# Expert rows stored in the tokens' order: plain loads instead of gathers, and shared experts in chunks of 256

## The reference

```
layer 1: h = norm(h + moe)   8 experts, top 2:  sum over e of gate[t,e] * (gelu(LN(x) w1[e] + b1[e]) w2[e] + b2[e])
layer 2: h = norm(h + moe)  16 experts, top 2:  sum over e of gate[t,e] * ((silu(x wg[e]) * (x wu[e])) wd[e])
                            + mean over s = 0, 1 of (silu(x shared_wg[s]) * (x shared_wu[s])) shared_wd[s]
layer 3: h = norm(h + moe)   8 experts, top 1:  p[t] * (relu(x wi[e]) wo[e])
```

## Time and profile before

| | |
|---|---|
| runs before | 2610.99, 2610.76, 2607.44 us, median 2610.76 |
| profiled execution | 2604.46 us, span on the core 2602.6 us, mean granted clock 0.884 |
| busy over the span | PE 2198.8 us (84%), DVE 1468.0 (56%), ACT 872.4 (34%), POOL 909.1 (35%) |
| bytes | HBM read 162.67 MB, written 63.28 MB |

### The profile page before, as it was taken

The page is one execution under the profiler, slowest core; times in us unless marked ns, Lnnn a source line. Parts: engine busy times, 40 slices in busy tenths (PEclk is TensorE's granted clock), DMA queues, the critical chain, the costliest instruction groups (busy, mean ns, idle before and its releaser), DMA issues. The chain is left out here.

```text
span 2602.6 us, 47198 instructions
## 1 busy us (share of the span) xinstructions
PE 2198.8 (84%) x17833; PEld 1944.9 (75%) x17833; DVE 1468.0 (56%) x3567; ACT 872.4 (34%) x1886; POOL 909.1 (35%) x828
## 2 busy tenths in 40 slices
PE   8999995689789858996998979998999995663598
PEld 7888884477678747994676769998999995552487
DVE  2676776746667764324999853332443226777424
ACT  0333435622244413333654431111111112576211
POOL 0333234700011062326777521310111116563546
PEclk9988996789999958998999989999999998755599
DMA  9500000070090055551000023001566651000354
GB/s 271 184 1 1 1 1 20 1 221 2 9 215 2 12 174 166 181 171 31 14 11 11 1 82 141 30 15 61 194 213 212 213 192 50 11 1 1 111 171 124
DMA packets 134490, 229.02 MB, mean 88 GB/s; under 512 B 15402, under 2 KB 105902, under 8 KB 127482
## 3 DMA queue, kind: packets, MB, share of 16 engines
q1 hardware_dynamic: 123642, 207.35, 25.1%
q0 software_dynamic: 10624, 18.66, 2.4%
HBM read 162.67 MB, written 63.28 MB: 87 GB/s over the span
## 5 line engine op out<-in xcount | busy, mean ns | idle before, releaser
L2623 POOL COPY bl_swiglu_w<-ahead_w2swiglu_w 128x1152 f32 x51 | 58.4, 1147 | 359.8 <-PE psum L2684 264.6
L2726 ACT ACTIVATE bl_swiglu_sg<-psum 128x384 f32<-128x384 f32 x102 | 50.0, 490 | 300.6 <-PE psum L2673 300.6
L2662 PE MATMUL psum<-bl_swiglu_xt,bl_swiglu_w 128*128 128x128 f32 x1224 | 147.3, 278 | 1.7 <-DVE bl_swiglu_hid L2763 1.1
L2662 PEld LDWEIGHTS psum<-bl_swiglu_xt,bl_swiglu_w 128*128 128x128 f32 x1224 | 145.5, 195 | 2.3 <-issue 2.3
L2753 DVE COPY bl_swiglu_xt<-psum 128x256 f32<-128x256 f32 x51 | 21.6, 424 | 198.4 <-PE psum L2643 198.4
L2623 POOL COPY bl_gelu_w<-ahead_w2gelu_w 128x1350 f32 x43 | 57.8, 1365 | 144.1 <-DVE bl_gelu_y L2785 131.0
L2738 ACT ACTIVATE bl_gelu_hid<-psum,bl_gelu_w 128x128 f32<-128x128 f32 x258 | 70.9, 377 | 110.4 <-POOL bl_gelu_w L2623 107.4
L2684 PE MATMUL psum<-bl_swiglu_w,bl_swiglu_hid 128*128 128x192 f32 x612 | 107.9, 327 | 0.0
L2988 ACT ACTIVATE shared_sg<-psum 128x432 f32<-128x432 f32 x66 | 35.0, 530 | 206.5 <-PE psum L2925 206.5
L2918 PE MATMUL psum<-tower_xT,shared_w 128*128 128x216 f32 x528 | 100.2, 347 | 0.6 <-ACT tower_xT L2982 0.6
L2684 PEld LDWEIGHTS psum<-bl_swiglu_w,bl_swiglu_hid 128*128 128x128 f32 x612 | 98.3, 191 | 0.1
(11 more groups left out here) (679 smaller groups left out, 6081.9 us busy)
## 6 DMA issues: line engine op xcount, KB each, us to landing
bl_swiglu_w<-in_swiglu_w SPq DMA_DIRECT2D x51, 1152.0 KB, 5.3
rows_in<-tower_fill SPq DMA_DIRECT2D x2, 13824.0 KB, 45.6
bl_gelu_w<-in_gelu_w SPq DMA_DIRECT2D x43, 576.0 KB, 4.1
bl_relu_w<-in_relu_w SPq DMA_DIRECT2D x25, 576.0 KB, 4.0
rows_last<-tower_fill SPq DMA_DIRECT2D x1, 14065.0 KB, 62.6
ahead_w2swiglu_w<-in_swiglu_w SPq DMA_DIRECT2D x1, 9216.0 KB
tok_x<-in_x SPq DMA_DIRECT2D x11, 648.0 KB, 12.5
ahead_w2gelu_w<-in_gelu_w SPq DMA_DIRECT2D x1, 5400.0 KB
```

What stands on the lines that cost most here:

```text
L2623: pool.tensor_copy(w2[:, n % DEEP], w2all[:, e, :].rearrange("p e n -> p (e n)")).then_inc(s_w2, 1)
L2662: pe.matmul(up_tile(n, j, i, side), w[:, o:o + 128], xt[:, n % 2, side, :], start=(i == 0), stop=False, skip_group_check=True)
L2726: act.activation(sg[:, j], bank_pair(n, j)[:, 0, 0:3 * BLOCK].rearrange("p (i n) -> p i n", i=3), ACT.Silu).then_inc(s_silu, 1)
```

## The change

- **One row format.** The DRAM array `rows_in` is 194 wide for all three layers and has one shelf more; `rows_last` and its clearing go. `h` gets a row pitch of 194 values. Column `NAME` of each row carries the token's number plus an epoch that differs by layer (`first_name`), `MORE` the first pick (relu: the factor).
- **Scatter in the blocks.** Gelu and SwiGLU lose SP's `store`. DVE computes for each of the 128 rows of a block where its result belongs (`addressed`): token number, plus 2304 if the row's expert is not the token's first pick; a row that holds no token of this layer goes to a spare row. POOL scatters `y` of block n - 4 behind its copy of block n. `y` has 4 buffers instead of 2. SP's next load of rows waits for the address step instead of the turn.
- **Plain loads in the combine.** `fetch` moves from POOL to SP: one transfer for a tile brings both results of its 108 tokens, two for the last tile. The first four stand ahead of all else in SP's stream of the stage. `slots`, `find_slots` and the slot arithmetic of the routes go; the block plan (`lay_blocks`) now runs on 128 partitions and also writes `mine`, the expert of each block on every partition.
- **Shared experts in chunks of 256.** 9 chunks for each expert, 18 iterations. Their sums are laid out by 128 rows, not by 108, so SP stores them to a DRAM array `rows_shared` and the SwiGLU stage loads them back in tiles of 108, behind the first three blocks' loads; `h` += `side` moves from block n to block n + 4. `GATES` moves from `NP + 6` to `NP + 5`.

The core of the diff:

```diff
@@ blocks, SP
                         if n >= XR:
-                            sp.wait_ge(c_y if last else p_T, n - XR + 1)
+                            sp.wait_ge(c_y if last else c_to, n - XR + 1)
...
                     S.arrived(sp, s_all)
+                    if glu:
+                        side, both = cst["side"], cst["both"]
+                        sp.wait_ge(cst["kept"], 16 * (TOK // (2 * BLOCK)))
+                        sp.dma_start(side[:, 0:NT - 1], both[0:(NT - 1) * T].rearrange("(t p) n -> p t n", p=T)).then_inc(cst["level"], 16)
...
                     for n in range(NB):
                         if n + DEEP < NB:
                             fetch_rows(n + DEEP)
                             fetch_weights(n + DEEP)
-                        if glu:
-                            store(n)
-                        elif n >= 3 and not last:
-                            store(n - 3)
@@ blocks, POOL
                     def scatter(n):
-                        x = n % KEPT
-                        pool.wait_ge(c_z, n + 1)
-                        pool.indirect_dma_start(out=cst["out"], out_offset=bass.IndirectOffsetOnAxis(ap=to[:, x:x + 1], axis=0),
+                        x, k = n % KY, n % KT
+                        pool.wait_ge(c_z if last else c_y, n + 1)
+                        pool.indirect_dma_start(out=out, out_offset=bass.IndirectOffsetOnAxis(ap=to[:, k:k + 1], axis=0),
                                                 in_=y[:, x, :], in_offset=None).then_inc(s_st[x], 16)
...
-                        if last and n >= 6:
-                            scatter(n - 6)
+                        if n >= LAG:
+                            scatter(n - LAG)
@@ blocks, DVE
                         ins.then_inc(c_T, 1)
+                        addressed(n)
+
+                    def addressed(n):
+                        x, k = xr[:, n % XR], n % KT
+                        if n >= KT:
+                            dve.wait_ge(s_st[n % KY], before[n % KY] + 16 * ((n - KT) // KY + 1))
+                        low = float(first - first_name(kind))
...
+                        K.then(dve.tensor_scalar(at[:, 0, k:k + 1], x[:, MORE:MORE + 1], cst["mine"][:, n:n + 1], float(TOK),
+                                                 ALU.not_equal, ALU.mult))
+                        K.then(dve.scalar_tensor_tensor(at[:, 1, k:k + 1], x[:, NAME:NAME + 1], low, at[:, 0, k:k + 1], ALU.add, ALU.add))
+                        dve.tensor_tensor(to[:, k:k + 1], at[:, 1, k:k + 1], cst["spare"][:, n:n + 1], ALU.max).then_inc(c_to, 1)
...
-                        if n >= 2:
-                            dve.wait_ge(s_st[n % 2], 16 * (n // 2))
+                        if n >= KY:
+                            dve.wait_ge(s_st[n % KY], before[n % KY] + 16 * (n // KY))
@@ combine
-    def fetch(self, pool, t):
+    def fetch(self, sp, t):
         if t >= WAY:
-            pool.wait_ge(self.added, self.TOP * (t - WAY + 1))
-        for c in range(self.TOP):
-            pool.indirect_dma_start(out=self.got[:, t % WAY, c, :], out_offset=None, in_=self.cst["ys"][0:self.rows],
-                                    in_offset=bass.IndirectOffsetOnAxis(ap=self.slots[:, c, t:t + 1], axis=0)
-                                    ).then_inc(self.landed[t % WAY], 16)
+            sp.wait_ge(self.added, self.TOP * (t - WAY + 1))
+        n, got, landed = own(t), self.got[:, t % WAY], self.landed[t % WAY]
+        sp.dma_start(got[0:n], self.rows[t * T:t * T + n]).then_inc(landed, 16)
+        if n < T:
+            sp.dma_start(got[n:T], self.rows[(t - 1) * T + n:t * T]).then_inc(landed, 16)
@@ shared
-    N = SHARED
+    N, W = SHARED, 2 * BLOCK
+    NC = TOK // W
...
-                                pe.matmul(up[j][:, part * 2 + i, 0:C], w[:, o:o + 128], xT[:, part, cols],
+                                pe.matmul(up[j][:, part * 2 + i, :], w[:, o:o + 128], xT[:, part, cols],
...
-                            ins = pe.matmul(dn[0:T, b, u, 0:D], hid[:, b, k, u * T:(u + 1) * T], w2[x][:, k, :],
+                            ins = pe.matmul(dn[:, b, u, 0:D], hid[:, b, k, u * BLOCK:(u + 1) * BLOCK], w2[x][:, k, :],
...
-                for n in range(N * NP):
-                    if n + 1 < N * NP:
+                for n in range(N * NC):
+                    if n + 1 < N * NC:
                         rise(n + 1)
                     fall(n)
@@ shared, SP
+                for c in range(NC):
+                    sp.wait_ge(s_acc, NC + c + 1)
+                    sp.dma_start(cst["both"][c * W:(c + 1) * W].rearrange("(u p) n -> p u n", p=BLOCK), acc[:, c]).then_inc(cst["kept"], 16)
```

More of the change, by code:

```diff
@@ L2124, in choose, with spare_rows, first_name, send_rows @@
     return ins
[L2127 to L2136 removed]
+def spare_rows(kind):
+    return block_count(kind) * BLOCK
+def first_name(kind):
+    return EPOCH * (1 + ("gelu", "swiglu", "relu").index(kind))
+def send_rows(pool, cst, rows, TOP, tiles):
     for t in tiles:
@@ L2819, in _ @@
                         lay(n)
-                        if glu and n < NT:
-                            dve.tensor_tensor(h[:, n, :], h[:, n, :], cst["side"][:, n, :], ALU.add)
+                        if glu and n == 4:
+                            dve.wait_ge(cst["level"], 48)
+                        if glu and 4 <= n < NT + 4:
+                            t = n - 4
+                            dve.tensor_tensor(h[:, t, :], h[:, t, :], cst["side"][:, t, :], ALU.add)
                     if last:
@@ L2833, in stage_shared @@
     HID, KC = 768, 6
-    N = SHARED
+    N, W = SHARED, 2 * BLOCK
+    NC = TOK // W
     E, TOP, NB = 16, 2, block_count("swiglu")
-    ident, side, xT = cst["ident"], cst["side"], cst["xT"]
-    gates, spots, slots, owner, place = [cst[k] for k in "gates spots slots owner place".split()]
-    wg, iota, before, ones, count, upto, steps = [
-        cst[k] for k in ("wgswiglu", "iota", "earlier", "ones", "count", "upto", "steps")]
+    ident, xT = cst["ident"], cst["xT"]
+    gates, spots, rows = cst["gates"], cst["spots"], cst["hw"]
+    wg, iota, before, ones, upto, steps = [cst[k] for k in ("wgswiglu", "iota", "earlier", "ones", "upto", "steps")]
     with Stage(nc, "shared", cst) as S:
@@ L3290, in _ @@
             def _(sp):
+                for t in range(WAY):
+                    C_.fetch(sp, t)
                 S.clear_before(sp)
+                for t in range(WAY, NT):
+                    C_.fetch(sp, t)
             @block.gpsimd
@@ L3831, in _ @@
                 for t in range(*rest.groups[0]):
-                    rest.level(pool, t, ends[:, t, 0:D])
+                    rest.level(pool, t)
                 rest.power(pool, 1)
@@ L4362, in _ @@
                 for t in range(*rest.groups[2]):
-                    rest.level(dve, t, ends[:, t, 0:D])
+                    rest.level(dve, t)
 def expert_layer(kind):
```

299 lines of the change are left out of this document (130 added, 169 removed).

## The result

| | before | after |
|---|---|---|
| median of the runs | 2610.03 us (2607.44 to 2610.99, 4 runs) | 2576.84 us (2574.93 to 2580.99, 4 runs) |
| ratio of after to before | | 0.9875, 95% interval 0.986 to 0.9891 |
| span of the profiled execution | 2602.6 us | 2575.2 us |

The change makes the kernel faster by 33.2 us (1.25%). Later runs of the unedited kernels add a second profile of before and two of after. From the first work of each stage to the first work of the next, in us. Three bounds differ: the first row starts with TensorE's first matmul, the last one ends with POOL's issue of the last scatter, and the turning of the tokens that opens the shared experts (6.2 us before, 6.9 to 7.4 after) is counted with spectral attention.

What follows compares the result with a forecast made beforehand. TensorE was taken to bound the shared experts and SwiGLU blocks, chains through POOL's gathers the combining stages. Terms -18.3 - 4 + 1 - 4 + 1 - 3 - 9 = -36.3 us gave a 2574 us median, range 2557 to 2593.

Steps and rivals of the forecast that it cites:

- Bound by stage: Whole kernel: TensorE bounds shared experts and SwiGLU blocks; POOL's gathers hold up spectral and quantised attention, TensorE next in the latter.
- Shared experts, -20.5 of TensorE's time and +2.2 of gates: Shared experts: 18 iterations of 12.12 us replace 22 of 10.85; the gates' DVE steps become an open tail; net -18.3 us.
- Blocks, 0: Gelu, SwiGLU and relu blocks: scatters and address steps fit into existing slack, 0 us; SwiGLU bound +10 us.
- The slower rival: SwiGLU blocks: address steps wait out POOL's scatter, delaying the multiply 0.93 us per block, 46 us in all; 2620 us, chance 0.05.
- The load of `side`: Start of SwiGLU blocks: reading 1.77 MB back ahead of the fourth weights costs 0 us, bound +4.
- Tails, +1 each, bounds 0 and +2.4: Ends of gelu and SwiGLU stages: ending on a scatter instead of SP's store costs +1 us each.
- Spectral attention, -4 at the start and -4 after: Spectral attention: ACT's second levelling waits less for POOL, -4 us; then 7 pairs gain 0.6 us each, -4 us.
- Quantised attention, -3 and -9: Quantised attention: second levelling comes earlier, -3 us; then 10 periods fall to 5.2 us, gaining 0.9 each, -9 us.
- Clears, 0 "under long stages": Clearing the extra rows: costed at nothing because the clears lie under long stages.
- "hidden gathers" rival: Spectral and quantised attention: gathers were already covered, so only shared experts (-18.3) and tails (+2) remain; 2594 us, chance 0.15.
- "more than I take" rival: Shared experts, spectral and quantised attention: each gain reaches its bound, tails still +1 each, -46.6 us; 2564 us, chance 0.12.

## Why the prediction was right, and where its steps were off

**Bound by stage.** Right: TensorE in the shared experts, POOL's gathers in the combining stages, and TensorE next behind them in the quantised one. The first two came out when one part alone was undone (20 to 24 and 22 to 25 us), the third shows in the periods above.

**Shared experts, -20.5 of TensorE's time and +2.2 of gates.** Measured -21.5 (243.68 to 222.14) and +2.3 (16.73 to 19.02). Scaling the rises by columns and leaving the fall alone gave 12.12 us for 12.06.

**Blocks, 0.** Right for the steady part of both: SwiGLU's 6.54 us a block stayed, with a slack of 0.13 us left, and gelu's 8.71 a pair. Only the first SwiGLU blocks lost 0.5 us, where the steps had no slack to hide in; with the 3.7 us of the tail that is the stage's 4.3, within 0.1. The slower rival needed a scatter to hold the steps. In the SwiGLU rows above the scatter runs from 2004.85 to 2005.82 and the steps from 2008.35 on, so they don't meet; in the gelu blocks some do, which the forecast doesn't weigh, and they are not held (rows in the last section). The load of `side`: 0, as taken.

**Tails, +1 each, bounds 0 and +2.4.** The step that failed most plainly. I took the copy, the scatter's issue and its landing for all that a stage's end waits for. Measured +2.2 and +3.7, the second beyond its bound, because POOL's queue closes 2.2 and 2.9 us after the transfer has landed; taking the scatters out gave both back. Why the drain lasts beyond the landing isn't shown.

**Spectral attention, -4 at the start and -4 after.** From the stage's first POOL work to the first tanh it is 24.7 us before and 22.0 after (20.5 in the third profile): -2.7 to -4.2. The steady part gave -7.3 instead of -4. The floor was read rightly, but I gave every pair the same 0.6: the four periods of 28.8 to 29.0 us gained 0.7 to 0.9 each, while the two behind them, 29.98 and 32.11 before, fell to 28.08 and 29.61. Another 2.2 to 3.3 us, which the forecast hasn't, came from the last tanh to the turning of the tokens (48.91 before, 46.73 and 45.60 after); with the gathers back it was 49.03.

**Quantised attention, -3 and -9.** From first work to last levelling 72.18 before, 58.67 after, -13.5. The second levelled pair follows the first after 2.81 us, 6.15 before, so -3.3 where -3 was forecast. The steady period is 4.82, not 5.2. The forecast read TensorE's 5.0 us from a stretch that is no whole number of periods; in one period it was 4.80. And the 0.2 us for other waits don't arise, as TensorE is busy for all of the 4.82.

**Clears, 0 "under long stages".** Very likely wrong for the second one. I checked that the transfers had time, not whether the work beside them kept its pace; with it the performer stage took 1 to 8 us more, 4.9 in the mean of the three profiles of after. The "hidden gathers" rival (2594) fell with the experiment that brought the gathers back, the "more than I take" rival (2564) was nearer for the gains (44.7 us in the three stages, against its 48.6 and the forecast's 38.3), but not for the costs. That the time came out within 3 us of 2574 is luck in so far as gains and costs were both put too low.

## What to carry to other kernels

Before moving a queue's work, look at what the issuing engine holds up: 88 gathers of a microsecond each, 44 in each of two stages, were worth over 20 us where a chain ran through POOL, and 94 scatters cost nothing in loops where POOL had room. Price the end of a stage separately from its loop, since an engine that issued indirect transfers last may close later than its data lands. A transfer "hidden under a long stage" is only free if the stage beside it takes the same time with and without it, so try it in another stage.

## What the runs showed of the hardware

The closing drain of POOL's queue took 4.78 and 5.43 us, and ended 2.2 and 2.9 us after SP had seen the last scatter land. With plain stores nothing of it shows: the whole gap was 2.2 us.

Tiny DVE steps do get held beside POOL's tensor work. At the start of the gelu blocks, after:

```profile
997.50 3.83 POOL L2615 COPY bl_gelu_w<-ahead_w2gelu_w 128x1350 f32 x3 [13.01 <-SPq L127]
...
999.34 0.73 DVE L2760 SCALAR_TENSOR_TENSOR bl_gelu_at<-bl_gelu_xr,bl_gelu_at 128x1 f32<-128x1 f32 x1
...
1000.11 1.22 DVE L2761 TENSOR_TENSOR bl_gelu_to<-bl_gelu_at,tower_spare 128x1 uint32<-128x1 f32 x1
```

The same two steps take 0.16 us each in the SwiGLU rows above. A POOL scatter doesn't hold them: in the gelu blocks of after 11 address steps run beside one, two of them with two SBUF inputs, all at their usual 0.16 or 0.20 us. One of these:

```profile
1066.55 0.98 POOL L2607 DMA_INDIRECT rows_out<-bl_gelu_y,bl_gelu_to  x1 [0.16 <-issue]
...
1067.46 0.16 DVE L2760 SCALAR_TENSOR_TENSOR bl_gelu_at<-bl_gelu_xr,bl_gelu_at 128x1 f32<-128x1 f32 x1
```

In the spectral attention the additions of result rows moved in time against POOL's work, and their durations with them (ns, least, median and longest), to be held against the earlier trace rows:

```profile
L2435 DVE SCALAR_TENSOR_TENSOR tower_h<-sp_got,tower_gates,tower_h x44: 401/1316/1719, 1200.7 to 1452.3; 108x192 f32<-108x192 f32 x44
...
L2435 DVE SCALAR_TENSOR_TENSOR tower_h<-qa_got,tower_gates,tower_h x44: 400/417/445, 2150.7 to 2198.2; 108x192 f32<-108x192 f32 x44
```

The longest fell from 6.8 to 1.7 us, the median rose from 0.42 to 1.32, and the stage still gained. The 6.8 us, from 1382.68 to 1389.46 before, lasted through five tensor instructions of POOL in a row. The Trainium skill ("SBUF — State Buffer", section "SBUF: two separate sides") says that a DVE operation with two SBUF inputs and a GpSimd operation that reads SBUF lock each other out of a shared port. The trace agrees for POOL's tensor work, whose copies and products read SBUF (0.73 to 6.8 us, as above).
